# Skip term, y and the low half of u moved off VectorE in the second layer of a two-layer kernel

## What is computed

```python
xs = jax.nn.silu((xc + conv1d_b[None, :, None]).transpose(0, 2, 1))
x_dbl = jnp.einsum('bld,rd->blr', xs, x_proj_w)
dt = jax.nn.softplus(jnp.einsum('blr,dr->bld', x_dbl[..., :DT_RANK], dt_proj_w) + dt_proj_b)
def step(h, inp):
    xt, dtt, Bt, Ct = inp
    dA = jnp.exp(dtt[..., None] * A)
    h = dA * h + dtt[..., None] * Bt[:, None, :] * xt[..., None]
    y = jnp.einsum('bdn,bn->bd', h, Ct)
...
return ys.transpose(1, 0, 2) + x * D
```

## Time and profile before

| | us |
|---|---|
| median of 3 runs | 5985.74 |
| lowest, highest | 5984.24, 5988.39 |
| profiled execution, its own time | 5988.07 |
| its span, first to last instruction | 5986.3 |

### The profile page before, as it was taken

The page is one execution under the profiler, slowest core; times in us unless marked ns, Lnnn a source line. Parts: engine busy times, 40 slices in busy tenths (PEclk is TensorE's granted clock), DMA queues, the critical chain, the costliest instruction groups (busy, mean ns, idle before and its releaser), DMA issues. The chain is left out here.

```text
span 5986.3 us, 84041 instructions
## 1 busy us (share of the span) xinstructions
PE 5515.8 (92%) x27184; PEld 2520.1 (42%) x27184; DVE 4841.2 (81%) x7122; ACT 3701.3 (62%) x7290; POOL 4207.8 (70%) x3213
## 2 busy tenths in 40 slices
PE   7999999999999999999999999968888878888887
PEld 4444444444444444444444444423333333333333
DVE  7777777777777777777777777639999999999999
ACT  3666666665666666666666666656666666666665
POOL 2767666677676677776667776638787887878787
PEclk8999999999999999999999999989999999999999
DMA  4011010110110101101010000024444444454444
GB/s 135 21 43 41 20 38 22 43 40 27 43 35 21 45 20 43 41 24 36 24 26 22 8 22 13 20 94 172 168 161 168 160 169 162 168 168 160 168 160 153
DMA packets 292503, 464.74 MB, mean 78 GB/s; under 512 B 72384, under 2 KB 95808, under 8 KB 290624
## 3 DMA queue, kind: packets, MB, share of 16 engines
q1 hardware_dynamic: 292064, 459.37, 23.6%
HBM read 381.41 MB, written 76.28 MB: 76 GB/s over the span
## 5 line engine op out<-in xcount | busy, mean ns | idle before, releaser
L560 POOL TENSOR_TENSOR sums<-exps 128x512 f32<-128x512 f32 x2048 | 2617.2, 1298 | 1313.2 <-ACT exps L493 1308.3
L569 DVE TENSOR_REDUCE mpart<-ps 128x1 f32<-128x512 f32 x4096 | 2541.6, 683 | 818.9 <-PE ps L369 818.9
L493 ACT ACTIVATE exps<-ps 128x512 f32<-128x512 f32 x4096 | 2127.9, 603 | 1404.0 <-PE ps L376 1403.6
L369 PE MATMUL ps<-k_st,q_ring 96*128 96x512 f32 x4096 | 1753.9, 429 | 17.3 <-DMA k_st<-qk_split 8.9
L1232 POOL TENSOR_TENSOR hc<-hh,c_rep 128x512 f32<-128x512 f32 x1024 | 1361.8, 1338 | 392.3 <-DVE hh L1195 391.9
L376 PE MATMUL ps<-q_ring,k_st 98*128 98x512 f32 x4096 | 1621.7, 397 | 4.0 <-ACT exps L493 3.6
L1195 DVE TENSOR_TENSOR_SCAN hh<-d_a,carry,ps 128x512 f32<-128x512 f32 x1024 | 1308.6, 1281 | 1.0
L369 PEld LDWEIGHTS ps<-k_st,q_ring 96*128 96x128 f32 x4096 | 775.1, 189 | 1063.4 <-DVE mpart L569 508.2
L387 PE MATMUL ps<-exps,v_ring 128*32 128x512 f32 x8192 | 1090.8, 605 | 0.0
L376 PEld LDWEIGHTS ps<-q_ring,k_st 98*128 98x128 f32 x4096 | 777.7, 190 | 148.4 <-ACT exps L493 17.3
L1021 PE MATMUL ps<-s_u,sel_g 128*128 128x512 f32 x1024 | 559.1, 549 | 199.0 <-DVE hh L1195 197.4
(11 more groups left out here) (106 smaller groups left out, 3075.4 us busy)
## 6 DMA issues: line engine op xcount, KB each, us to landing
d_a<-dt_dram SPq DMA_DIRECT2D x1040, 256.0 KB
qk_split<-hilo SPq DMA_DIRECT2D x128, 256.0 KB, 2.3
q_ring<-qk_split SPq DMA_DIRECT2D x384, 64.0 KB, 2.0
k_st<-qk_split SPq DMA_DIRECT2D x45, 512.0 KB, 7.1
dt_dram<-dt SPq DMA_DIRECT2D x33, 512.0 KB, 2.8
za<-z_ext SPq DMA_DIRECT2D x33, 320.0 KB, 3.8
zp<-z_ext SPq DMA_DIRECT2D x32, 320.0 KB, 6.6
xc<-in_x SPq DMA_DIRECT2D x32, 256.0 KB, 3.0
```

Source lines behind the costliest of these rows:

```text
L369: nc.tensor.matmul(d_bank(("max", m, t)), q_ring[0:PARTS, m % 4, 128 * i:128 * i + 128], k_st[0:PARTS, g % 2, chunk(kc)], start=True, stop ...
L493: nc.scalar.activation(exps[:, u % 4, CH * half:CH * half + CH], a_bank(("exp", n, t)), ACT.Exp, scale=SCALE).then_inc(a_done, 1)
L560: pool.tensor_tensor(sums[:, u % 8, :], exps[:, u % 4, 0:CH], exps[:, u % 4, CH:2 * CH], ALU.add).then_inc(summed, 1)
L569: nc.vector.tensor_reduce(mpart[:, m % 2, t % 4, t // 4:t // 4 + 1], d_bank(("max", m, t)), AX.X, ALU.max).then_inc(d_done, 1)
```

## The change

Four parts, all in `layer1`:

1. The skip term xs x D becomes the first product of each y sum: a 128x128 matrix with D on the diagonal (`wskip`, loaded once, 128 KB) times xs, in full float32. y is then read from PSUM by ScalarE with a plain copy (`read_y`): half 0 at step 23, half 1 at step 10 of the next chunk, behind that step's exponential and carry copy. `add_skip` is gone.
2. ScalarE writes the rounded u once in its own layout (`hi_u`, 128x1024) at step 23, and the two high halves of `s_u` together at step 24.
3. GpSimd subtracts: `lo_u` = u - `hi_u`, 128x1024, at step 23.
4. The two halves of `lo_u` are placed into `s_u` by two DMAs of 256 KB, issued by ScalarE at step 30 once `lo_ready` is there. TensorE's `repeat_u` waits for both (`u_placed`) at step 0. ScalarE's silus at step 9 wait for the sums themselves (`y_done`) instead of `y_added`.

```diff
+        hi_u = sb("hi_u", [128, 2, LC], F32R)
+        lo_u = sb("lo_u", [128, 2, LC], F32R)
+        wskip = sb("wskip", [128, 2, 128])
...
+                sp.wait_ge(u_placed, 32 * (NIT + 1))
...
                     if n % 4 == 0:
                         ge(pe, y_added, it * 2 + n // 4)
+                        nc.tensor.matmul(ps[:, Y_BANK, :], wskip[:, n // 4, :], xs[:, it % 2, n // 4, :], start=True, stop=False)
                     for i in range(4):
                         ins = nc.tensor.matmul(ps[32 * i:32 * i + 32, Y_BANK, :], sel_y[:, n % 4, :], hc[:, (4 * n + i) % NHC, :],
-                                               start=(n % 4 == 0), stop=(n % 4 == 3))
+                                               start=False, stop=(n % 4 == 3))
...
                     if g == 0:
-                        pe.wait_ge(lo_ready, it * 2 + 2)
+                        pe.wait_ge(hi_ready, it * 3 + 3)
+                        pe.wait_ge(u_placed, it * 32 + 32)
...
-                def high(j, p, stack, src, part):
+                def high(p, part):
                     a = slice(64 * part, 64 * part + 64)
-                    nc.scalar.copy(stack[a, p, part::2, :], src[a, :, :]).then_inc(hi_ready, 1)
+                    nc.scalar.copy(s_u[a, p, part::2, :], ux[a, :, :]).then_inc(hi_ready, 1)
+
+                def place_low(j, p):
+                    act.wait_ge(lo_ready, j + 1)
+                    for part in range(2):
+                        a, b = slice(64 * part, 64 * part + 64), slice(64 - 64 * part, 128 - 64 * part)
+                        act.dma_start(s_u[b, p, part::2, :].bitcast(F32), lo_u[a, :, :].bitcast(F32)).then_inc(u_placed, 16)
+
+                def read_y(it, half):
+                    act.wait_ge(y_done, it * 8 + 4 * half + 4)
+                    ge(act, o_ready, it)
+                    nc.scalar.copy(yt[:, half, :], ps[:, Y_BANK, :]).then_inc(y_added, 1)
...
-                        ge(act, y_added, j * 2 - 2)
+                        ge(act, y_done, j * 8 - 8)
                         silus(xs[:, p, :, :], j, XS, lambda h: cols[:, h:h + 1])
...
-                    elif g in (23, 24):
+                    elif g == 23:
                         act.wait_ge(u_prod, j + 1)
-                        high(j, p, s_u, ux, g - 23)
+                        ge(act, lo_ready, j)
+                        nc.scalar.copy(hi_u[:, :, :], ux[:, :, :]).then_inc(hi_ready, 1)
+                    elif g == 24:
+                        for part in range(2):
+                            high(p, part)
+                    elif g == 30:
+                        place_low(j, p)
...
+                        if g == 23:
+                            read_y(it, 0)
+                        if g == 10 and it:
+                            read_y(it - 1, 1)
                         prepare(it + 1, 1 - p, g)
...
+                    elif g == 23:
+                        pool.wait_ge(hi_ready, j * 3 + 1)
+                        ge(pool, u_placed, j * 32)
+                        pool.tensor_tensor(lo_u[:, :, :], ux[:, :, :], hi_u[:, :, :].bitcast(F32), ALU.subtract).then_inc(lo_ready, 1)
```

## The result

The changed kernel takes **6164.06 us** (median of 4 runs, 6157.13 to 6169.97) against 5986.19 us of the kernel before on the same chip: ratio 1.0296, 95% interval 1.0282 to 1.0311. Slower by 178 us. I had forecast 5992 us, and a range up to 6050 us.

The account below looks back on a forecast made before the run. VectorE bounds the kernel at 61.4 us a chunk; the bound moves to a loop of 59.4 us, plus 2.2 for the clock, 61.6. Over 31 chunks that adds 6 us: 5994, less 2.3 for the median, 5992; range 5920 to 6050.

Parts of the forecast that it names:

- the ceiling 57.0: VectorE's chunk without skip sums and low-half subtractions: 57.0 us, 4.4 less, a gain of at most 136 us.
- ScalarE's extra copy makes groups 25 and 28 late: The hi_u copy, 1.0 us, delays ScalarE's exponentials, so VectorE waits 0.65 at group 25 and 0.6 at 28.
- GpSimd to the copy, 5.9: From the start of GpSimd's dt sum through its product u to the start of ScalarE's copy: 5.9 us.
- The copy to the issue, 11.9: From ScalarE's copy of u to its DMA issue, after the exponentials of group 28 and later: 11.9 us.
- The transfers, 3.3, between 2.8 and 4.3: DMAs placing u's low half: 3.3 us, chosen between dt's store, 2.8, and za's load plus second issue, 4.3.
- TensorE, ScalarE, TensorE to the product of group 9: From placed u through conv1d products, silu and copy of y to the spreading for group 9: 11.6, 3.3 and 2.4 us.
- 2.2 for the clock: Loss from TensorE's clock falling after its waits for u and at group 8: 2.2 us a chunk, bounds 0 and 5.4.
- VectorE to the next dt sum, 21.0: From VectorE's product by B of group 9 through scan 18 and GpSimd's hc to the next dt sum: 21.0 us.
- the loop: Chain through all engines from one dt sum to the next: 59.4 us a chunk, above VectorE's own 58.25.
- The one on the slow side: Rival: TensorE's clock falls at the wait for u in every chunk, 3.4 us each, 6030 us; chance 0.25.
- The rule of the Trainium skill: A loop where TensorE waits for a DMA every pass drops to half clock every pass; chunk at least 62.8 us.
- the rival with the greatest chance beside mine: TensorE's clock holds or its falls are covered, so the 59.4 us chunk rules: 5924 us; chance 0.33.

Follow-up runs that it names:

- e10: e7 with TensorE's state sum of step 0 moved to step 2, behind the spreading for groups 1 and 2; 5857.30 us.
- e5: The change, with SyncE waiting before its load at step 19 until u's low half is placed; 6090.43 us, of two runs.
- e7: The change without transfers: GpSimd writes both low parts straight to place, ScalarE's high halves as before the change, y's second half read at step 8; 5958.37 us.

## Why the prediction was wrong

The forecast was no change, 5992 us; the kernel is slower by 178 us, and outside the range. Point by point, with the chunk of the rows above, from dt's sum at 5325.92 to the next at 5393.48, 67.6 us (GpSimd's rows):

```profile
5325.92 2.37 POOL L1224 TENSOR_TENSOR dt<-dt,edt 128x1024 f32<-128x1024 f32 x1
...
5393.48 2.35 POOL L1224 TENSOR_TENSOR dt<-dt,edt 128x1024 f32<-128x1024 f32 x1
```

- *VectorE is the bound, its work between scans worth 4.4 us a chunk, the ceiling 57.0.* Right: e10 reaches 57.2.
- *ScalarE's extra copy makes groups 25 and 28 late by 0.65 and 0.6.* Right: 0.65 and 0.52.
- *GpSimd to the copy, 5.9.* 5.94 (5325.92 to 5331.86).
- *The copy to the issue, 11.9.* It is 9.7 to the first (5341.60) and 10.4 to the second. I had let the issue wait until the three exponentials ahead of it ended; it started with the first of them. This term was 2.2 too large.
- ***The transfers, 3.3, between 2.8 and 4.3.* This is the step that failed.** The term counts from the first issue, and from there it is 10.4: 7.1 too small. The prediction took the nearest row by kind and size, a store in a quiet moment, and for the upper end za's load with 0.5 added. Alone the transfers would have taken 4.6 from the first issue (e5), 0.3 above the upper end. But they were not alone: they stand in the stretch in which SyncE catches up on d_a, and there the two queues share what one of them already uses (180 and 188 GB/s). The sum has no term for the other queue beyond za's row. A row of before for just this stretch existed and I passed it over, the store of the output, issued at 5216.93 within the catch-up: 256 KB in 6.2 us.

```profile
out<-o_sb SPq DMA_DIRECT2D x32, 256.0 KB, 6.2
```

- *TensorE, ScalarE, TensorE to the product of group 9: 11.6 + 3.3 + 2.4 = 17.3, and 2.2 for the clock, 19.5.* It is 20.5 (5351.99 to 5372.45). What is above the 17.3 is 3.2 instead of 2.2; the two sums of 1.94 and 1.93 instead of 1.06 are 1.8 of it. **The clock falls behind the wait for u in every chunk**, and in this one at group 8 too, as in 17 of the 31. 0.92 of full over the long stretch is 2 x 0.08 x 67 = 10.7 us a chunk at half clock, but a good part of it lies in the waits themselves. This is the second term that was too small, by 1.
- *VectorE to the next dt sum, 21.0.* It is 21.03.

The sum with the measured terms is 5.94 + 9.74 + 10.39 + 20.46 + 21.03 = 67.6 us. So the loop was the right mechanism and the bound moved to it. Of the 6.0 us between 61.6 and 67.6, the transfers with their issue are 20.1 instead of 15.2, 4.9 (the transfers 7.1 more, the issue 2.2 less: one error took back a third of the other), and the clock 1.0. This chunk is one with both falls of the clock; over all, 31 periods of 67.0 instead of 61.6 are 167 of the 172 us between forecast and result.

*The rivals.* The one on the slow side, with 0.25 of the chance and 6030 us, was right in what it says of the clock, a fall in every chunk, but this is the smaller part of the loss; it named slow transfers only as a helper, with 1.0 more. (Its +43 us give 6029, not the 6035 written there; the 6030 stands.) The rule of the Trainium skill that stands behind it, from "TensorE: Matmul & The Clock Gate", section "HAM oscillation", held: here TensorE waits for a DMA in every chunk, the clock fell behind that wait in 31 of 31, and it was 0.92 over 2000 us against 0.97 before. That the clock holds, the rival with the greatest chance beside mine, did not happen.

*The range* ended at 6050 because it took the bounds of the transfers from rows that did not bound them. The store's 6.2 with the 0.5 of the second issue would have given 59.4 + 3.4 + 2.2 = 65.0 us and some 6097 us: an upper end that says slower, but still short of the result. No row of before has two queues at once, which is what the 10.4 came from.

## What to carry to other kernels

Work taken off the bound engine is worth what it adds between that engine's steps, and only if the new path lets nobody who works in a fixed order wait longer. A transfer in such a path is to be priced by rows of the same stretch, with what the other queues do in just that stretch, not by a row from a quiet moment; and before a transfer is used to move data between partitions, see whether an engine can write it there directly (here 126 us less). Then look at the order within an in-order engine: one copy two steps earlier gave 77 and 70 us, one sum two steps later 101 us (5958.37 to 5857.30).

## What was not expected of the hardware

- Two DMA queues of the same core moved 180 GB/s together over 8 us where one alone moved 188 right behind it, at a busy share of the DMA engines of 0.67 and 0.50; so a share of half was no free room for this mix. Why it is so was not found: the same trace has 248 GB/s in another stretch, and pieces of 4 KB gave 0.5 us of 9.3.
- ScalarE's DMA issue did not wait for the exponentials just ahead of it in the program: it started at 5341.60, with the exponential that started at 5341.58, while two more stood ahead of it. In e5 it is the same (5357.73 and 5357.72). It did stand behind the silus and the table load, though `lo_u` had been ready since 5340.3.
- GpSimd writes 64 partitions x 1024 elements to the other 64 partitions in 2.35 and 2.37 us (e7), the time of its 128x1024 subtraction (2.37). So writing to other partitions costs nothing extra, but an instruction on 64 partitions does half the work in the same time.
